# Mixed network on one Trainium2 core: the second tails of the expert rows written at the dense network's chunks 0 to 3 in place of 1, 3, 5 and 7

## The chip, the cores and the metric

One core of a Trainium2 chip runs the whole program. The metric is the time of one execution on the device in microseconds; runs are repeated and their median is compared.

## What is computed

The reference takes 16 sequences of 256 tokens with 128 features and passes them through four residual layers: a linear attention with two decays, a mixture of experts, a retention, and two layers of local attention with a gated feed-forward. The change lies in the mixture of experts, which is in short:

```python
probs = softmax(x_flat @ Wr.T)
topk_scores, topk_experts = top_k(probs, 2)            # two experts a token
y_fb = _ffn(x_flat, fw1, fb1, fw2, fb2)                # the dense network, for overflowing tokens
for e in range(8):
    idx = the first cap tokens that chose e            # cap = 1.25 * T * 2 / 8 = 1280
    y_e = _ffn(x_flat[idx], W1[e], b1[e], W2[e], b2[e])
    y_flat = y_flat.at[idx].add(y_e * w[:, None])
    y_flat = where(overflow, y_fb, y_flat)
```

## The kernel before

All 4096 tokens stay on the chip, features in the partitions, as the residual `XT` and the normed input `H`, in 8 chunks of 512 tokens. The mixture of experts is three blocks of code (`experts`): `routing`, `expert_layers`, `combine`. Each block is one program per engine, and a barrier of all engines closes it.

`routing` (L614) does four things.

- It loads the weights of the nine networks (eight experts and the dense one) and splits each in a high and a low part.
- It computes the routing on VectorE: for each token its two experts, their scores `w1` and `w2`, and the two row numbers `dst` in a table `expert_slots` in DRAM.
- It brings the tokens' rows to DRAM. `tok_rows` has one row of 130 numbers per token: 128 features, the weight, and the address at which the expert's result goes back. GpSimd (L720 to L727) issues 64 indirect DMAs, called scatters below, of 128 rows each: first the 32 blocks of tokens for the first choice (`c` = 0), then the same 32 for the second (`c` = 1). Between the passes the rows differ only in their last two columns. `tail(c, q)` (L829) writes these two columns for the quarter `q`, eight blocks of tokens, with two small copies on VectorE (L831, L832), and counts `tails`. GpSimd waits for `tails` before each group of eight scatters. Since the second tail overwrites the first, it must wait until the first pass's eight scatters of that quarter have landed; that is the semaphore `sent[0][q]`.
- It runs the dense network over the 8 chunks, three matmuls for each product (high and low parts, L689 and L705). ScalarE applies the Gelu (`Gf`, L766) and copies the overflow mask (`WEf`, L774), VectorE splits the result (`Gf_hi` L854, `Gf_lo` L856) and the next input (`Hf_lo` L842), and closes a chunk with `Zf` (L866) and the addition to `XT` (L869). The work is a pipeline: VectorE closes chunk c after splitting chunk c+1, TensorE puts chunk c+1's first product ahead of chunk c's second.

The four tails of the first pass are written before the dense network starts. Those of the second stand in VectorE's program behind the closing of a chunk, and that is where the change is:

```python
                    V.tensor_tensor(k.XT[:, chunk(c)], k.XT[:, chunk(c)], Z[:], ALU.add).then_inc(added, 1)
                    if c % 2:
                        dve.wait_ge(sent[0][c // 2], 16 * 8)
                        tail(1, c // 2)
```

Engines execute their programs in order, and the order is the one written. At the end of `routing` GpSimd waits for all scatters of the second pass, and `expert_layers` (L875) begins with the load of the first expert's rows (`xin`, L901) on SyncE's queue.

Of the kernel before, what the change touches and what calls it, by code (L numbers as in the profile page):

```python
# [58 lines left out]
def chunk(c):  # L59
    return bass.ds(c * CH, CH)  # L60
# [553 lines left out]
def routing(k, w, wide):  # L614
# [3 lines left out]
    with ExitStack() as ctx:  # L618
# [23 lines left out]
        sent = [[sem(f"sent{c}_{q}") for q in range(4)] for c in range(2)]  # L642
# [5 lines left out]
        @block.sync  # L648
        def _(sp):
            for i, (n, e) in enumerate(pieces):  # L650
                if i >= 4:
                    sp.wait_ge(w_lo, i - 3)
                part = k.dram[n][:, e, :] if n == "w1e" else k.dram[n][:, e, :, :].rearrange("p a b -> p (a b)")
                sp.dma_start(raw[:, i % 4, :], part).then_inc(raw_in[i % 4], 16)
                if i < 2:
                    sp.dma_start(w[("b1e", "b2e")[i]][:], k.dram[("b1e", "b2e")[i]]).then_inc(small_in, 16)
            sp.wait_ge(small_in, 32)
# [118 lines left out]
        @block.vector  # L776
        def _(dve):
            V = nc.vector
            done = [0]

            def after(ins):

                done[0] += 1
                ins.then_inc(step, 1)
                dve.wait_ge(step, done[0])

            dve.wait_ge(k.late_in, 16 * N_LATE)
            V.memset(fb, 0.0)
            V.memset(one, 1.0)
            V.memset(before[:, 0:1], 0.0)  # L790
            dve.wait_ge(logit_mm, 1)
            lg = ps[0][:, 0:NT * NE].rearrange("p (n e) -> p n e", e=NE)
            after(V.tensor_reduce(mx, lg, AX.X, ALU.max))
            V.tensor_tensor(pr[:], lg, bc(mx), ALU.subtract).then_inc(shifted, 1)
            dve.wait_ge(exped, 1)
            after(V.tensor_reduce(sm, pr[:], AX.X, ALU.add))
            after(V.reciprocal(rs_, sm))
            after(V.tensor_tensor(pr[:], pr[:], bc(rs_), ALU.mult))
            for p_, v_, hot in ((p1, v1, oh1), (p2, v2, oh2)):
                after(V.tensor_reduce(p_, pr[:], AX.X, ALU.max))  # L800
                after(V.tensor_tensor(eq[:], pr[:], bc(p_), ALU.is_equal))
                after(V.tensor_tensor(val[:], eq[:], r["iota8"][:], ALU.mult))
                after(V.tensor_reduce(v_, val[:], AX.X, ALU.min))
                after(V.tensor_tensor(hot[:], r["iota8"][:], bc(v_), ALU.is_equal))
                if hot is oh1:
                    after(V.scalar_tensor_tensor(pr[:], oh1[:], -2.0, pr[:], ALU.mult, ALU.add))
            after(V.tensor_tensor(oh[:], oh1[:], oh2[:], ALU.add))

            for e in range(NE):
                V.tensor_tensor(elig[:], oh[:, :, e], fb, ALU.is_gt).then_inc(elig_r, 1)  # L810
                dve.wait_ge(elig_r, 2 * e + 1)
                V.tensor_tensor_scan(before[:, 1:NT + 1], one, elig[:], 0.0, ALU.mult, ALU.add).then_inc(elig_r, 1)
                dve.wait_ge(counted, e + 1)
                after(V.scalar_tensor_tensor(over, ps[1][:, e * NT:(e + 1) * NT], float(CAP), elig[:], ALU.is_gt, ALU.mult))
                after(V.tensor_tensor(fb, fb, over, ALU.max))

            after(V.tensor_tensor(val[:], ps[1][:, 0:NE * NT].rearrange("p (e n) -> p n e", n=NT), r["slotbase"][:], ALU.add))
            for c, hot in enumerate((oh1, oh2)):
                after(V.tensor_tensor(eq[:], val[:], hot[:], ALU.mult))
                after(V.tensor_reduce(slot, eq[:], AX.X, ALU.add))  # L820
                after(V.scalar_tensor_tensor(dst[:, c, :], fb, float(NE * CAP), slot, ALU.mult, ALU.add))
            after(V.tensor_copy(fbb[:], fb))
            after(V.tensor_tensor(sm, p1, p2, ALU.add))
            after(V.tensor_scalar(sm, sm, 1e-9, None, ALU.max))
            after(V.reciprocal(rs_, sm))
            V.tensor_tensor(w1, p1, rs_, ALU.mult)
            after(V.tensor_tensor(w2, p2, rs_, ALU.mult))

            def tail(c, q):  # L829
                cc = slice(8 * q, 8 * q + 8)  # L830
                V.tensor_copy(tok[:, cc, P:P + 1].rearrange("p n o -> p (n o)"), (w1, w2)[c][:, cc])  # L831
                V.tensor_copy(tok[:, cc, P + 1:P + 2].rearrange("p n o -> p (n o)").bitcast(mybir.dt.uint32),  # L832
                              r["tokid"][:, c, cc]).then_inc(tails, 1)

            dve.wait_ge(tok_sb, NCH)
            for q in range(4):
                tail(0, q)
            dve.sem_inc(routed, 1)

            def split_low(c):  # L840
                dve.wait_ge(h_hi, c + 1)
                V.tensor_tensor(Hp[1][:, c % 2, :], k.H[:, chunk(c)], Hp[0][:, c % 2, :].bitcast(F32),  # L842
                                ALU.subtract).then_inc(h_lo, 1)

            split_low(0)
            split_low(1)
            for i in range(NCH + 1):
                if i < NCH:
                    for j in range(NJ):
                        n = NJ * i + j  # L850
                        dve.wait_ge(gelu, n + 1)
                        if i > 1 and j == 0:
                            dve.wait_ge(y_mm, i - 1)
                        V.tensor_scalar(Gp[0][:, i % 2, j, :], G[:, j, :], 1.0, None, ALU.mult).then_inc(g_hi, 1)  # L854
                        dve.wait_ge(g_hi, n + 1)
                        V.tensor_tensor(Gp[1][:, i % 2, j, :], G[:, j, :], Gp[0][:, i % 2, j, :].bitcast(F32),  # L856
                                        ALU.subtract).then_inc(g_lo, 1)
                    if i + 2 < NCH:
                        split_low(i + 2)
                if i > 0:  # L860
                    c = i - 1
                    dve.wait_ge(y_mm, c + 1)
                    dve.wait_ge(mask_sb, c + 1)
                    if c > 0:
                        dve.wait_ge(added, c)
                    V.scalar_tensor_tensor(Z[:], ps[4 + c % 2][:], w["b2e"][:, NE:NX], WE[:, c % 2, :],  # L866
                                           ALU.add, ALU.mult).then_inc(z_r, 1)
                    dve.wait_ge(z_r, c + 1)
                    V.tensor_tensor(k.XT[:, chunk(c)], k.XT[:, chunk(c)], Z[:], ALU.add).then_inc(added, 1)  # L869
                    if c % 2:  # L870
                        dve.wait_ge(sent[0][c // 2], 16 * 8)
                        tail(1, c // 2)


def expert_layers(k, w, wide):  # L875
# [1104 lines left out]
```

## Time and profile before

| | before |
|---|---|
| median of 3 runs | 1860.79 us |
| lowest and highest | 1853.89 and 1862.79 us |
| profiled execution, its own time | 1877.42 us |
| its span | 1875.6 us |
| TensorE busy | 1393.1 us (74%) |
| VectorE busy | 1249.4 us (67%) |
| ScalarE busy | 869.0 us (46%) |
| GpSimd busy | 729.5 us (39%) |
| granted TensorE clock, mean | 0.87 |

The durations come from one profiled execution; a difference worked out from them is set against the median of the others. The shares are means over stages of different kind, so they say little about one block. Of use are the order of time of one engine, with the idle time before each instruction and what ended it, and the table of stretches. The engines are written PE (TensorE), PEld (its weight loads), DVE (VectorE), ACT (ScalarE), POOL (GpSimd) and SP (SyncE); a q behind the name is the engine's queue.

### The profile page before, as it was taken

Reading aid. Unit: us, or ns where it says so; the run is one execution under the profiler, and the core shown is the slowest. Engines: PE = TensorE matmul, PEld = TensorE weight load, DVE = VectorE, ACT = ScalarE, POOL = GpSimd, SP = SyncE. Lnnn points to the kernel's source line nnn. Section 1 sums busy time; section 2 is a strip of 40 time slices with the busy share of each in tenths; the row PEclk is TensorE's granted clock in tenths of the full one; section 3 lists DMA queues with packets and bytes.
Section 4 is the critical chain, followed back from the end, with each engine's and each line's share of the span. In section 5 each row is a group of like instructions: output and inputs, shape, how many; then the busy total and the mean of one; then the engine's idle time right before and its main releaser. Section 6 shows DMA issues by size and latency. Waiting matters only on the chain. (4 is left out here: it accounts for less than half of the span.)

```text
span 1875.6 us, 24395 instructions
## 1 busy us (share of the span) xinstructions
PE 1393.1 (74%) x6912; PEld 885.8 (47%) x6912; DVE 1249.4 (67%) x2733; ACT 869.0 (46%) x1621; POOL 729.5 (39%) x588
## 2 busy tenths in 40 slices
PE   7756563674639882874888888888758888888887
PEld 3222121253428671322566666663336666667533
DVE  1598988337538771536988888844469888887343
ACT  6411111443325540563566666654326666666543
POOL 0287778026635553224433333301145333332000
PEclk9867776876669995985899999999959999999898
DMA  5400000021121214000000000000000000000001
GB/s 158 145 0 0 0 0 0 0 69 57 41 70 48 61 47 125 8 0 18 1 2 2 0 0 1 0 25 0 17 1 1 2 2 1 1 1 0 1 0 45
DMA packets 50658, 44.44 MB, mean 24 GB/s; under 512 B 5870, under 2 KB 43763, under 8 KB 50560
## 3 DMA queue, kind: packets, MB, share of 16 engines
q1 hardware_dynamic: 45952, 34.91, 6.4%
q0 software_dynamic: 4608, 8.47, 1.4%
q8 instruction: 32, 0.52, 0.1%
q14 instruction: 66, 0.54, 0.1%
HBM read 23.28 MB, written 21.12 MB: 24 GB/s over the span
## 5 line engine op out<-in xcount | busy, mean ns | idle before, releaser
L1385 POOL TENSOR_TENSOR R<-R 128x512 f32<-128x512 f32 x128 | 159.4, 1266 | 400.3 <-DVE R L1658 400.3
L1658 DVE TENSOR_TENSOR R<-bank,tab 128x1024 f32<-128x1024 f32 x128 | 151.6, 1221 | 55.4 <-ACT sq L1561 47.4
L1392 POOL TENSOR_TENSOR R<-R,rn 128x512 f32<-128x512 f32 x128 | 139.9, 1114 | 12.1 <-issue 10.0
L1498 PE MATMUL bank<-PT,VA 128*128 128x192 f32 x512 | 137.8, 352 | 0.0
L1561 ACT ACTIVATE sq<-bank 128x512 f32<-128x512 f32 x128 | 76.2, 597 | 122.4 <-PE bank L1410 117.3
L1436 PE MATMUL bank<-ident,R 128*128 128x128 f32 x512 | 85.3, 293 | 64.0 <-ACT VA L1584 61.9
L1677 DVE TENSOR_SCALAR QKr<-QK 128x512 fp32r<-128x512 f32 x128 | 92.6, 751 | 48.5 <-ACT QK L1577 47.0
L1034 POOL DMA_INDIRECT expert_rows<-Yt,xin x80 | 83.2, 1041 | 92.2 <-DVE Yt L1007 67.9
L1697 DVE TENSOR_TENSOR OT<-bank,rd 64x256 f32<-64x256 f32 x256 | 106.3, 415 | 19.1 <-ACT rd L1603 16.5
L1595 ACT ACTIVATE PT<-bank 128x320 f32<-128x320 f32 x256 | 98.0, 435 | 16.4 <-PE bank L1486 13.5
L1436 PEld LDWEIGHTS bank<-ident,R 128*128 128x128 f32 x512 | 61.6, 147 | 90.8 <-issue 47.0
L395 PE MATMUL bank<-phk,spread 128*128 128x512 f32 x64 | 45.9, 883 | 77.7 <-DVE phq L445 77.7
L463 DVE TENSOR_TENSOR_SCAN S<-beta,U 128x512 f32<-128x512 f32 x64 | 101.8, 1600 | 1.1
L1499 PE MATMUL bank<-PT,VA 128*128 128x128 f32 x512 | 101.0, 280 | 0.0
L1410 PE MATMUL bank<-wqkv_hi,hs_hi 128*128 128x512 f32 x128 | 62.9, 492 | 48.2 <-DVE hs_lo L1645 40.6
L1499 PEld LDWEIGHTS bank<-PT,VA 128*128 128x128 f32 x512 | 93.8, 197 | 0.0
L1688 DVE CUSTOM_DVE_ANT_0 masked<-bank,mask_q 128x192 bf16<-128x192 f32 x256 | 89.9, 351 | 0.0
L1577 ACT ACTIVATE QK<-bank 128x512 f32<-128x512 f32 x128 | 75.7, 593 | 26.0 <-PE bank L1436 26.0
L1498 PEld LDWEIGHTS bank<-PT,VA 128*128 128x128 f32 x512 | 81.6, 198 | 9.5 <-issue 6.7
L1601 ACT ACTIVATE rd<-bank 64x512 f32<-64x512 f32 x128 | 75.9, 593 | 17.0 <-PE bank L1499 14.2
L1603 ACT ACTIVATE rd<-rd 64x512 f32<-64x512 f32 x128 | 80.7, 630 | 4.1
L723 POOL DMA_INDIRECT expert_slots<-tok_rows,dst x64 | 64.4, 1006 | 43.7 <-DVE tok_rows L832 25.5
(306 smaller groups left out, 3877.2 us busy)
## 6 DMA issues: line engine op xcount, KB each, us to landing
expert_slots<-empty SPq DMA_DIRECT2D x8, 650.0 KB, 6.5
xin<-expert_slots SPq DMA_DIRECT2D x8, 650.0 KB
expert_rows<-empty SPq DMA_DIRECT2D x8, 512.0 KB, 6.7
Ye<-expert_rows SPq DMA_DIRECT2D x16, 256.0 KB, 5.3
expert_raw<-w1e_dram SPq DMA_DIRECT2D x9, 256.0 KB, 2.9
expert_raw<-w2e_dram SPq DMA_DIRECT2D x9, 256.0 KB, 3.0
tok<-x_dram SPq DMA_DIRECT2D x8, 256.0 KB, 4.6
out_dram<-tok_out SPq DMA_DIRECT2D x8, 256.0 KB, 3.3
```

Source lines behind the costliest of these rows:

```text
L463: nc.vector.tensor_tensor_scan(S[i % 2][:], beta[m][:, chunk(c)], U[d][:], 0.0, ALU.mult, ALU.add).then_inc(s_scan, 1)
L1034: nc.gpsimd.indirect_dma_start(k.ys[:, :], bass.IndirectOffsetOnAxis(ap=ids, axis=0), Yt[:, s % 3, t, :], None, bounds_check=2 * T - 1, oo ...
L1385: nc.gpsimd.tensor_tensor(halves[:, :, 0, :, z, :], halves[:, :, 0, :, z, :], halves[:, :, 1, :, 1 - z, :], ALU.add).then_inc(summed, 1)
L1392: nc.gpsimd.tensor_tensor(x, x, scale.to_broadcast([P, HEADS, DH]), ALU.mult).then_inc(normed, 1)
L1436: m = nc.tensor.transpose(ps[bank][:, b * P:(b + 1) * P], R[:, t % 2, qk, 0, b * P:(b + 1) * P], k.const["ident"][:])
L1498: nc.tensor.matmul(bank[:, o:o + KW], VA[par][:, 2 * s, h, :], pt[:, 0:KW], start=True, stop=True)
L1499: nc.tensor.matmul(bank[:, o + P:o + SEQ], VA[par][:, 2 * s + 1, h, :], pt[:, KW:KW + P], start=False, stop=True, skip_group_check=True).t ...
L1595: nc.scalar.activation(PT[:, u % 4, :], ps[BT + u % 2][:, 0:KW + P], ACT.Exp, scale=QK_SCALE).then_inc(pt_r, 1)
L1658: nc.vector.tensor_tensor(R[:, i, qk, :, :].rearrange("p c (h d) -> p c h d", d=DH), x, y.to_broadcast([P, 2, HEADS, DH]), ALU.mult).then_ ...
L1677: nc.vector.tensor_scalar(QKr[cc], QK[par][cc], 1.0, None, ALU.mult).then_inc(qkr_r, 1)
L1688: nc.vector.tensor_tensor_reduce(masked[:, v % 2, KW:2 * KW], bank[:, KW:2 * KW], mask[:, KW:2 * KW], -1.0, FAR, ALU.add, ALU.min, nm[:, 2 ...
L1697: m = nc.vector.tensor_tensor(OT[par][i * DH:(i + 1) * DH, b, s * SEQ:(s + 1) * SEQ], ps[BO + p % 2][0:DH, i * SEQ:(i + 1) * SEQ], rd[:, p ...
```

## The change

The second tails are written behind chunks 0, 1, 2 and 3 of the dense network, one quarter each, where they stood behind chunks 1, 3, 5 and 7.

```diff
@@ -867,9 +867,9 @@
                     V.tensor_tensor(k.XT[:, chunk(c)], k.XT[:, chunk(c)], Z[:], ALU.add).then_inc(added, 1)
-                    if c % 2:
-                        dve.wait_ge(sent[0][c // 2], 16 * 8)
-                        tail(1, c // 2)
+                    if c < 4:
+                        dve.wait_ge(sent[0][c], 16 * 8)
+                        tail(1, c)
```

On VectorE, behind the closing of chunk 0 in the dense network (a minus is a row of before alone, a plus one of the change; `cols` holds the scores, `tokid` the addresses):

```order
 L866 SCALAR_TENSOR_TENSOR Zf<-bank,b2e,WEf 128x512
 L869 TENSOR_TENSOR XT<-XT,Zf 128x512
+L831 COPY tok_rows<-cols 128x8
+L832 COPY tok_rows<-tokid 128x8
 L854 TENSOR_SCALAR Gf_hi<-Gf 128x512
 L856 TENSOR_TENSOR Gf_lo<-Gf,Gf_hi 128x512
```

The two copies of the first quarter now stand ahead of the splitting of chunk 2. The same piece stands behind chunk 2 for the third quarter. Behind chunks 1 and 3 the rows read the same before and after, though the quarter is another one: the second in place of the first, the fourth in place of the second.

On VectorE, behind the closing of chunk 7, at the end of the block (L618 is the block's end):

```order
 L866 SCALAR_TENSOR_TENSOR Zf<-bank,b2e,WEf 128x512
 L869 TENSOR_TENSOR XT<-XT,Zf 128x512
-L831 COPY tok_rows<-cols 128x8
-L832 COPY tok_rows<-tokid 128x8
 L618 UNCONDITIONAL_BRANCH
```

The last quarter's copies have left this place, and those behind chunk 5 likewise. The order on the other engines is unchanged.

## Rows read from the trace of the kernel before

**Rows 1.** Table of stretches: busy time of each engine, clock, DMA.
```profile
core 0: us, PE busy (x) PEld busy (x) DVE busy (x) ACT busy (x) POOL busy (x), PEclk, DMA share, GB/s
445.00:462.00 17.00, 16.44 (x68) 12.71 (x68) 11.95 (x20) 6.79 (x11) 12.95 (x13) 0.87 0.14 46
462.00:492.00 30.00, 7.38 (x18) 4.07 (x18) 7.35 (x12) 4.42 (x7) 19.21 (x20) 0.57 0.14 45
492.00:527.00 35.00, 32.44 (x140) 24.24 (x139) 32.97 (x65) 17.16 (x29) 21.73 (x22) 0.93 0.12 40
527.00:552.00 25.00, 0.00 (x0) 0.00 (x0) 0.00 (x0) 0.00 (x0) 10.50 (x11) 0.52 0.22 63
```
**Rows 2.** POOL in order of time: start, us, instruction, idle before and releaser.
```profile
445.39 1.67 POOL L723 DMA_INDIRECT expert_slots<-tok_rows,dst  x1 [12.98 <-DVE tok_rows L832]
...
455.27 0.97 POOL L723 DMA_INDIRECT expert_slots<-tok_rows,dst  x1 [0.30 <-issue]
...
486.03 0.97 POOL L723 DMA_INDIRECT expert_slots<-tok_rows,dst  x1 [0.30 <-issue]
493.81 1.12 POOL L723 DMA_INDIRECT expert_slots<-tok_rows,dst  x1 [6.81 <-DVE tok_rows L832]
...
507.74 1.12 POOL L723 DMA_INDIRECT expert_slots<-tok_rows,dst  x1 [3.59 <-DVE tok_rows L832]
...
520.16 1.12 POOL L723 DMA_INDIRECT expert_slots<-tok_rows,dst  x1 [2.08 <-DVE tok_rows L832]
...
539.57 0.97 POOL L723 DMA_INDIRECT expert_slots<-tok_rows,dst  x1 [0.30 <-issue]
```
**Rows 3.** The block's end, line L618: duration in ns min/median/max, start in us.
```profile
L618 DVEq DRAIN  x1: 879/879/879, 526.0 to 526.0; - x1
...
L618 POOLq DRAIN  x1: 5285/5285/5285, 542.5 to 542.5; - x1
```
**Rows 4.** All engines in order of time, from 540 us on.
```profile
547.98 2.92 SPq L901 DMA_DIRECT2D xin<-expert_slots  x3
...
552.35 0.90 PE L913 MATMUL bank<-ident,xin 128*128 128x128 f32 x3 [27.63 <-DMA xin<-expert_slots]
```
**Rows 5.** DVE in order of time.
```profile
462.44 0.75 DVE L866 SCALAR_TENSOR_TENSOR Zf<-bank,b2e,WEf 128x512 f32<-128x512 f32 x1 [3.29 <-PE bank L705]
...
491.40 0.75 DVE L866 SCALAR_TENSOR_TENSOR Zf<-bank,b2e,WEf 128x512 f32<-128x512 f32 x1 [5.32 <-remote]
...
492.87 0.17 DVE L832 COPY tok_rows<-tokid 128x8 uint32<-128x8 uint32 x1
...
497.88 0.74 DVE L866 SCALAR_TENSOR_TENSOR Zf<-bank,b2e,WEf 128x512 f32<-128x512 f32 x1
...
505.33 0.75 DVE L866 SCALAR_TENSOR_TENSOR Zf<-bank,b2e,WEf 128x512 f32<-128x512 f32 x1 [0.83 <-remote]
...
525.22 0.75 DVE L866 SCALAR_TENSOR_TENSOR Zf<-bank,b2e,WEf 128x512 f32<-128x512 f32 x1
...
526.69 0.17 DVE L832 COPY tok_rows<-tokid 128x8 uint32<-128x8 uint32 x1
```
**Rows 6.** ACT in order of time.
```profile
466.67 0.69 ACT L766 ACTIVATE Gf<-bank,b1e 128x512 f32<-128x512 f32 x1 [11.61 <-remote]
470.96 0.69 ACT L766 ACTIVATE Gf<-bank,b1e 128x512 f32<-128x512 f32 x1 [3.60 <-remote]
...
483.59 0.69 ACT L766 ACTIVATE Gf<-bank,b1e 128x512 f32<-128x512 f32 x1 [5.62 <-remote]
...
490.60 0.60 ACT L774 ACTIVATE WEf<-bank 128x512 f32<-128x512 f32 x1 [5.81 <-remote]
491.45 2.42 ACT L766 ACTIVATE Gf<-bank,b1e 128x512 f32<-128x512 f32 x4 [0.25 <-remote]
```
**Rows 7.** PE in order of time: first and last matmul of chunk 2's first product, 12 in all.
```profile
456.03 0.39 PE L689 MATMUL bank<-Hf_hi,w1e_hi 128*128 128x512 f32 x1
...
458.59 0.40 PE L689 MATMUL bank<-Hf_hi,w1e_lo 128*128 128x512 f32 x1
```
**Rows 8.** Waits of ACT over the whole span: us in total, times, longest.
```profile
ACT Yf L974 <- remote: 35.6, 7, 8.6
```

## The prediction, made before the kernel was run

> **What bounds the kernel at this place.** I read the table of stretches first [rows 1]. The dense network runs from 445 to 527 us of the span, TensorE, VectorE and ScalarE are empty from 527 to 552, and GpSimd alone still works there. The program ends each block of code with a barrier of all engines, so the question is who arrives last. GpSimd's order of time answers it [rows 2]: it issues 64 scatters of rows, in a first pass of 32 (445.39 to 487.00) and a second of 32 that it begins at 493.81 and ends at 540.54. Its drain takes 5.29 us [rows 3], the queue issues the first load of the experts at 547.98, and TensorE, idle for 27.63 us, starts at 552.35 [rows 4]. From the end of the last scatter to that load it is 7.4 us. All later work stands behind that load, so a microsecond won or lost at the barrier is one of the kernel's.
>
> The second pass has holes. GpSimd waits for VectorE's second tails (weight and address of the rows) for 6.81 us, 3.59 us and 2.08 us; the fourth tail is in time [rows 2]. A scatter costs 0.30 us of idling in any case, so the holes are worth 12.48 - 3 x 0.30 = **11.6 us**. That is all that writing tails earlier can give.
>
> Why are tails late? VectorE's rows [rows 5] give the chunk's first closing operation (Zf): chunk 0 at 462.44, chunk 1 at 491.40, chunk 2 at 497.88, chunk 3 at 505.33, chunk 7 at 525.22. Between chunks 2 to 7 it is 5.5 us on average; between 0 and 1 it is 29 us. In those 29 us ScalarE's Gelus and one copy come one at a time, 4 to 7 us apart, at 466.67, 470.96, 483.59 (one more lies between) and 490.60, and then four follow without a pause [rows 6]. The matmuls that they wait for were shown long before: chunk 2's group runs from 456.03 to 458.98 and needs nothing more, while the Gelu on its first bank starts at 466.67 [rows 6, 7]. So TensorE's results become known late, one by one, in this stretch. GpSimd scatters without a pause from 445.39, the results are first late after some 10.6 us of that (456.03), and all are released by 491.40, 4.4 us after the last scatter of the pass ended. The wait that the profile calls "remote" falls where GpSimd scatters, also in the expert layers (7 waits of Yf, 35.6 us) [rows 8]. I read this as one fact: a long stream of scatters holds TensorE's results up, and a pause in the stream releases them. Why it does is not in the rows.
>
> **The change, step by step.** It moves two copies of 128x8 each (0.17 us each in rows 5) and one wait, four times, on VectorE alone; no other engine's order changes, and nothing is added.
>
> 1. *Tail 1 goes from behind chunk 1 to behind chunk 0.* Its wait is for the first eight scatters, the last of which was issued at 455.27 and generated by 456.2 [rows 2]. Bounding the landing by the drain, 5.3 us [rows 3], it is satisfied by 461.5; chunk 0 closes at 462.44. No stall, and the tail is written at 464, long before GpSimd wants it at 487.3. The first hole closes: group 1 of the second pass runs from 487.3 to 497.6 (eight scatters take 10.3 us, from 41.6 us for 32 in the first pass and 20.4 us for 16 at the end).
> 2. *Tail 2 goes from behind chunk 3 to behind chunk 1.* In before, chunk 1 closed at 491.40 because the stream had stopped. Now the stream goes on to 497.6. If the release needs the stop, chunk 1 closes at 497.6 + 4.4 = 502.0, its tail is ready 1.6 us later (as 491.40 to 493.04) and GpSimd starts 0.8 us after that (493.04 to 493.81), at 504.4. **A hole of 6.8 us stands again, one group later.** Group 2 runs to 514.7. If instead chunk 1 still closes at 491.40, or by 496, there is no hole.
> 3. *Tail 3, from behind chunk 5 to behind chunk 2.* Chunk 2 follows chunk 1 by 6.5 us [rows 5]: 508.5, tail 510.1, before 514.7. No hole; group 3 runs from 515.0 to 525.3.
> 4. *Tail 4, from behind chunk 7 to behind chunk 3.* Chunk 3 follows chunk 2 by 7.45 us: 515.9 if nothing is late. But the stream that began at 504.4 reaches 10.6 us of age at 515.0, just then. The ends are 515.9 and 525.3 + 4.4 = 529.7. The tail stands at 517.5 to 531.3, so group 4 starts between 525.6 and 532.1 and ends between 535.9 and 542.4. With the 7.4 us up to the load: 543.3 to 549.8.
> 5. *The rest of the network.* In before it takes 21.5 us from chunk 3's Zf to the last tail (505.33 to 526.86) [rows 5], and VectorE's drain 0.9 us [rows 3]. Counted from 515.9 or 529.7 the network is at the barrier at 538.3 or 552.1. Its cover, the 21 us by which VectorE was early at the barrier, is used up at the late end.
>
> Sum: the load goes out at the later of both, 543.3 to 552.1 against 547.98, which is **-4.7 to +4.1 us**, centre 0. The waits that the change adds on VectorE cost nothing in this sum: each asks for eight scatters of the first pass, over by 487.0 and landed by 492.3, while chunk 1 closes at 491.4 or later and chunk 3 far behind. What queues behind such a wait is chunk c+1's Gf_hi, and TensorE waits for that.
>
> **Against the median.** The profiled execution took 1877.42 us (span 1875.6), 16.6 us above the median of 1860.79. The sum is a difference, and I take it from the median: 1860.8 + 0, said as **1861 us**.
>
> **Rivals.**
> - *N, nothing was late outside the profiled execution.* The 16.6 us may include the late results themselves; the rows cannot tell. Then chunks follow at 6.5 us from chunk 0's 462.4 on, the four tails of before stand at 470.5, 483.5, 496.5 and 509.5 and are wanted at 487, 498, 508 and 518: GpSimd has no hole to close. After the change VectorE waits for landings in chunks 1 to 3, until about 492 at most; chunks 4 to 7 add 26 us, 518, still ahead of GpSimd's 528. The change does nothing: 0 us, 1861.
> - *F, all the holes close.* Chunks 1, 2 and 3 closed at 491.4, 497.9 and 505.3 in before; group ends are 497.6, 507.9 and 518.2. If the network keeps its own pace whatever GpSimd issues, all tails are in time and the full 11.6 us come: 1849.2. For it: the release at 490.60 also fits the 6 to 7 us steps before it and need not come from the stop. Against it: in one step after 490.60 everything was free, which a plain step does not explain. The Trainium skill, SBUF — State Buffer, § Who interferes with whom, supports F: it says that only VectorE and GpSimd share ports and that TensorE and ScalarE never wait on anyone. By that rule the scatters would not hold up TensorE and the sum would be -11.6 us; rows 6 and 7 do not look like it.
> - *S, slower: the network is held one chunk per group.* If results are late again sooner than 6.5 us into group 2 (the deciding point: chunk 2 not closed by about 513), then chunk 2 closes at 514.7 + 4.4 = 519.1, group 3 starts at 521.5 and stops at 531.8, chunk 3 closes at 536.2, group 4 ends at 548.9 and the load goes out at 556.3; the network is at the barrier at 536.2 + 21.5 + 0.9 = 558.6. That is +10.6 us, 1871.4. For it: groups now follow each other with shorter pauses, so the hold-up may not empty. Against it: in before, 2 to 3.6 us of pause between groups kept chunks at 7.5 us or less.
>
> **How the numbers follow.** My case has 0.40, N 0.25, F 0.17, S 0.18. A measurement of this kernel can tell about 0.5%, 9.3 us, from no change. F is over it by 2 us only and S by 1.3, so each gives its side about 0.12 and leaves the rest within; the edges of my case add 0.03 to faster and 0.06 to slower. Faster 0.15, same 0.67, slower 0.18. The range reaches to F at 1849 and to S at 1872: beyond it lies half of F and of S.
>
> **What would show it.** In the profile after: the first second-pass scatter directly behind the 32nd of the first (idle 0.30 us); then one hole of 5 to 8 us before the 9th, ended by L832; chunk 1's Zf near 502 and not 491; the last scatter's end between 536 and 543. Zf of chunk 1 at 491 or before with scatters unbroken to 528 would be F. Three holes again, with chunk 2 behind 513, would be S. If the load stands earlier in the profile but the median does not move, N is right. I am wrong altogether if VectorE idles before L831 for a landing, or if a later stretch changes its length.

## The result: 0.3% slower, with one hole in place of three

| | before | changed kernel |
|---|---|---|
| median of 20 runs each | 1859.15 us (1853.89 to 1867.22) | 1866.55 us (1857.50 to 1871.15) |
| ratio to before, 95% interval | | 1.0030 (1.0019 to 1.0041), about +5.6 us |
| profiled execution, its span | 1877.42, 1875.6 | 1867.42, 1865.1 |
| granted TensorE clock, mean of the span | 0.870 | 0.873 |
| first load of the experts | 547.98 | 552.46 |

By the prediction's measure of 0.5% this is no difference; the interval says that it is a small loss all the same. The profiled execution of after is shorter than that of before by 10 us while the median is longer by 7: the experts' layers after the load took 176.3 us in the profiled execution of before and 163.3 us in this one (from the load to the end of that block), and the change touches nothing there. So spans are not compared below, but the place where the load goes out.

The stretches of the changed kernel, in the columns of [rows 1] (length, busy time and instructions of PE, PEld, DVE, ACT and POOL, granted clock, DMA share, GB/s):

```profile
445.00:462.00 17.00, 16.16 (x68) 12.67 (x68) 13.75 (x26) 6.71 (x11) 12.67 (x13) 0.87 0.13 43
462.00:492.00 30.00, 9.81 (x24) 5.36 (x23) 5.31 (x11) 3.86 (x6) 22.99 (x24) 0.58 0.16 52
492.00:527.00 35.00, 24.52 (x89) 16.76 (x89) 19.11 (x39) 10.85 (x18) 21.62 (x22) 0.74 0.13 42
527.00:552.00 25.00, 13.66 (x46) 9.16 (x45) 14.08 (x24) 6.64 (x11) 6.80 (x7) 0.64 0.07 22
```

The last stretch, in which before had only GpSimd at work, now holds the end of the dense network: TensorE is busy for 13.66 us of it. GpSimd's scatters, the four that matter (against [rows 2]):

```profile
486.58 0.97 POOL L723 DMA_INDIRECT expert_slots<-tok_rows,dst  x1 [0.30 <-issue]
...
496.79 0.97 POOL L723 DMA_INDIRECT expert_slots<-tok_rows,dst  x1 [0.30 <-issue]
504.90 1.12 POOL L723 DMA_INDIRECT expert_slots<-tok_rows,dst  x1 [7.15 <-DVE tok_rows L832]
...
534.83 0.97 POOL L723 DMA_INDIRECT expert_slots<-tok_rows,dst  x1 [0.30 <-issue]
```

The second pass follows the first without a hole, one hole of 7.15 us stands before its ninth scatter, and the last scatter ends at 535.80 (before: 540.54). GpSimd is 4.7 us earlier. The network is not. VectorE's closing operations of chunks 1, 2, 3, 4, 5 and 7 (against [rows 5]):

```profile
502.49 0.75 DVE L866 SCALAR_TENSOR_TENSOR Zf<-bank,b2e,WEf 128x512 f32<-128x512 f32 x1 [23.45 <-remote]
...
508.98 0.74 DVE L866 SCALAR_TENSOR_TENSOR Zf<-bank,b2e,WEf 128x512 f32<-128x512 f32 x1
...
515.50 0.74 DVE L866 SCALAR_TENSOR_TENSOR Zf<-bank,b2e,WEf 128x512 f32<-128x512 f32 x1
...
531.84 0.75 DVE L866 SCALAR_TENSOR_TENSOR Zf<-bank,b2e,WEf 128x512 f32<-128x512 f32 x1 [9.73 <-remote]
...
542.80 0.74 DVE L866 SCALAR_TENSOR_TENSOR Zf<-bank,b2e,WEf 128x512 f32<-128x512 f32 x1
...
550.70 0.75 DVE L866 SCALAR_TENSOR_TENSOR Zf<-bank,b2e,WEf 128x512 f32<-128x512 f32 x1 [0.78 <-PE bank L705]
```

Chunk 4 comes 16.3 us behind chunk 3. In before that step had no wait. ScalarE shows the same two hold-ups (against [rows 6]), each ended some 3 to 5 us after GpSimd's last scatter of a run (497.76 and 535.80), with several Gelus at once:

```profile
502.54 2.42 ACT L766 ACTIVATE Gf<-bank,b1e 128x512 f32<-128x512 f32 x4 [16.98 <-remote]
...
519.16 0.60 ACT L774 ACTIVATE WEf<-bank 128x512 f32<-128x512 f32 x1 [2.87 <-remote]
534.65 0.69 ACT L766 ACTIVATE Gf<-bank,b1e 128x512 f32<-128x512 f32 x1 [14.90 <-remote]
538.88 1.84 ACT L766 ACTIVATE Gf<-bank,b1e 128x512 f32<-128x512 f32 x3 [3.54 <-remote]
```

The drains of the block's end, and then the load (against [rows 3, 4]): the three drain figures are minimum, median and maximum in ns, then the start.

```profile
L618 POOLq DRAIN  x1: 5285/5285/5285, 537.6 to 537.6; - x1
...
L618 DVEq DRAIN  x1: 727/727/727, 551.5 to 551.5; - x1
```

```profile
552.46 2.98 SPq L901 DMA_DIRECT2D xin<-expert_slots  x3
...
556.89 1.11 PE L913 MATMUL bank<-ident,xin 128*128 128x128 f32 x4 [6.22 <-DMA xin<-expert_slots]
```

GpSimd is drained at 542.9, VectorE at 552.2. The barrier waited for GpSimd in before; now it waits for the network. That is the load's +4.5 us between the two profiles, and it is most of the measured 5.6.

The waits by name also show where the time of a hold-up is booked (engine, line, releaser; total, times, longest):

```profile
ACT Gf L766 <- remote: 54.7, 7, 17.0
...
DVE Zf L866 <- remote: 34.2, 3, 23.4
...
ACT Yf L974 <- remote: 13.0, 5, 4.0
```

Gf and Zf waited 27.5 and 6.2 us in before and wait 54.7 and 34.2 us now; Yf, in the experts, fell from 35.6 to 13.0 us, which is the profiled execution's own difference named above. What TensorE itself does in a hold-up, from its order of time: the last matmul of chunk 1's second product, and then chunk 2's second product between 488 and 501:

```profile
461.94 0.40 PE L705 MATMUL bank<-Gf_hi,w2e_lo 128*128 128x512 f32 x1
...
489.85 0.59 PE L705 MATMUL bank<-Gf_hi,w2e_lo 128*128 128x512 f32 x1 [0.81 <-issue]
492.65 0.59 PE L705 MATMUL bank<-Gf_hi,w2e_hi 128*128 128x512 f32 x1 [2.21 <-issue]
495.45 0.59 PE L705 MATMUL bank<-Gf_lo,w2e_hi 128*128 128x512 f32 x1 [2.21 <-issue]
498.25 0.59 PE L705 MATMUL bank<-Gf_hi,w2e_lo 128*128 128x512 f32 x1 [2.21 <-issue]
500.35 0.59 PE L705 MATMUL bank<-Gf_hi,w2e_hi 128*128 128x512 f32 x1 [1.51 <-issue]
```

From 489.85 to 498.25 it is one matmul in 2.8 us, its weight load in between, so one instruction in 1.4 us; the matmuls of the same product just before (485.99 to 487.41) follow each other at 0.42 to 0.57 us. The idle time is put down to "issue", a wait for nothing that the profile shows. The step shortens again with this weight load, 0.70 us behind the matmul at 498.25 and 1.2 us after the scatters stopped:

```profile
498.95 0.29 PEld L705 LDWEIGHTS bank<-Gf_hi,w2e_hi 128*128 128x128 f32 x1 [1.82 <-issue]
```

So two things happen. Finished results become known late, as the prediction had it, and this is what chunk 1 waited for: its last matmul began at 461.94 and its Zf started at 502.49, 40 us later. On top of that, TensorE's instructions are spaced out after a while, here those of chunk 2. Before the spacing began TensorE had run ahead of the results that were known: by an estimate from the order of the matmuls, 32 lay between the last known result (the mask of chunk 1, copied at 484.97) and the last one at full pace (487.41), and 33 at the second hold-up (519.16 and 521.17).

### The profile page after: what moved, and what is told of

Same layout as the page of the kernel before. It is cut to its first block and busy times, and to the rows that moved or that the text cites. A ratio compares the mean times of both kernels' runs of the same rounds, so it can differ in the third digit from the quotient of the medians.

```text
span 1865.1 us, 24395 instructions
## 1 busy us (share of the span) xinstructions
PE 1393.6 (75%) x6912; PEld 887.2 (48%) x6912; DVE 1251.2 (67%) x2733; ACT 869.0 (47%) x1621; POOL 727.4 (39%) x588
## 5 line engine op out<-in xcount | busy, mean ns | idle before, releaser
L1595 ACT ACTIVATE PT<-bank 128x320 f32<-128x320 f32 x256 | 98.0, 435 | 16.6 <-PE bank L1486 13.8
L1686 DVE CUSTOM_DVE_ANT_0 masked<-bank,mask_q 128x128 bf16<-128x128 f32 x256 | 73.0, 285 | 11.8 <-issue 4.8
```

The lines of the kernel that those rows point to most:

```text
L1595: nc.scalar.activation(PT[:, u % 4, :], ps[BT + u % 2][:, 0:KW + P], ACT.Exp, scale=QK_SCALE).then_inc(pt_r, 1)
```

## Experiments

Twelve runs in five series. Each series ran on another chip, with runs of before on the same chip beside it. The theory after the result, called **held up**: a long unbroken stream of scatters holds TensorE up (its results are known late and, later on, its instructions are spaced out), and the change exchanges two short pauses for a second hold-up. Rivals: **pace** (the scatters have nothing to do with it, the network is slow there), **landing** (what counts is the transfers in flight, not the stream of issues) and **null** (nothing is late in most executions).

**1. Before, once more, with a profile.**

> The kernel before once more, for a second trace. Theory A (a stream of scatters holds TensorE up; the changed kernel is slower because its network now ends last at the barrier): the first load of the experts at 548 us of the span again, chunk 1's Zf at 491, and the experts' block of code, 176 us in the first trace of before and 163 us in the trace after, is near 163 us here, so that the first trace of before was an outlier there. Rival B (the change shortens the experts' block by 13 us and something else costs more): 176 us again.

Measured 1846.97 us; the median of before beside it on that chip was 1845.53 us (11 runs), not 1860. VectorE, GpSimd, and the load:

```profile
457.28 0.74 DVE L866 SCALAR_TENSOR_TENSOR Zf<-bank,b2e,WEf 128x512 f32<-128x512 f32 x1
463.83 0.74 DVE L866 SCALAR_TENSOR_TENSOR Zf<-bank,b2e,WEf 128x512 f32<-128x512 f32 x1
...
497.38 0.75 DVE L866 SCALAR_TENSOR_TENSOR Zf<-bank,b2e,WEf 128x512 f32<-128x512 f32 x1
```

```profile
491.30 0.97 POOL L723 DMA_INDIRECT expert_slots<-tok_rows,dst  x1 [0.30 <-DVE tok_rows L832]
...
525.81 0.97 POOL L723 DMA_INDIRECT expert_slots<-tok_rows,dst  x1 [0.30 <-issue]
```

```profile
533.94 2.99 SPq L901 DMA_DIRECT2D xin<-expert_slots  x3
```

The same program on another chip has no late result at all: chunks 6.5 us apart, no wait for "remote" anywhere in its list of waits, the 64 scatters without a hole, the load 14.0 us earlier. Its stretch from 462 to 492, in the columns used above:

```profile
462.00:492.00 30.00, 28.54 (x136) 21.19 (x134) 29.22 (x58) 17.21 (x28) 22.99 (x24) 1.00 0.16 52
```

Same 24 scatters, same DMA share and GB/s as in after's row of that stretch, but 136 matmuls against 24, and the granted clock at 1.00, the level of 2.4 GHz, where the changed kernel's TensorE idled for two thirds of the stretch and had 0.58. Theory A's places of the load (548) and of chunk 1's Zf (491) were missed; its 163 us for the experts' block came out as 157.8. This split the question in two: what holds TensorE up, and where it happens. Below, a chip with hold-ups is one where the median of before lies near 1860 us, as in the result, and not near 1845. Each chip was met in one series only, so a chip and its session are not told apart.

**2. One unbroken stream: GpSimd writes the second tails itself (on before).**

```diff
                     if n % 8 == 0:
+                        if c:
+                            q = n // 8
+                            pool.wait_ge(sent[0][q], 16 * 8)
+                            nc.gpsimd.tensor_copy(tok[:, n:n + 8, P:P + 1].rearrange("p n o -> p (n o)"), w2[:, n:n + 8])
+                            nc.gpsimd.tensor_copy(tok[:, n:n + 8, P + 1:P + 2].rearrange("p n o -> p (n o)").bitcast(mybir.dt.uint32),
+                                                  r["tokid"][:, 1, n:n + 8]).then_inc(tails, 1)
                         pool.wait_ge(tails, 4 * c + n // 8 + 1)
...
-                    if c % 2:
-                        dve.wait_ge(sent[0][c // 2], 16 * 8)
-                        tail(1, c // 2)
```

> GpSimd writes the second tails itself, so that no scatter waits for VectorE and the 64 scatters are one stream. Theory A: TensorE is held from about 456 us to the end of the stream; scatters end at about 535 us (82 us, plus four pairs of small copies), chunk 1's Zf comes 4 to 5 us after that, about 539, and the remaining six chunks take some 36 us: load of the experts at about 575, 27 us later than in before, time about 1886 us, if the hold-up is there in timed runs too. Rival F (the network keeps its pace): the load at about 542, time 6 us under before. Rival N (the hold-up is of the profiled execution only): 1886-like spans in the profile, but timed runs at or under before's.

Measured 1850.12 us (8 runs), ratio 1.0032 (1.0015 to 1.0048). GpSimd pays for the copies at each group (here 0.79 us instead of 0.30 before a group, and the copies):

```profile
488.64 0.28 POOL L725 COPY tok_rows<-cols 128x8 f32<-128x8 f32 x1
488.87 0.39 POOL L726 COPY tok_rows<-tokid 128x8 uint32<-128x8 uint32 x1
490.05 1.08 POOL L729 DMA_INDIRECT expert_slots<-tok_rows,dst  x1 [0.79 <-POOL tok_rows L726]
```

From its first scatter to the load it is 93.9 us, 90.4 in experiment 1: the copies cost 3.6 us, within the interval of 2.8 to 8.9. There was no hold-up here, so it said nothing of one.

**3. No scatters at all (on before).**

```diff
-            for c in range(2):
-                for n in range(NT):
-                    if n % 8 == 0:
-                        pool.wait_ge(tails, 4 * c + n // 8 + 1)
-                    nc.gpsimd.indirect_dma_start(k.xs[:, :], bass.IndirectOffsetOnAxis(ap=dst[:, c, n:n + 1], axis=0),
-                                                 tok[:, n, :], None, bounds_check=NE * CAP - 1,
-                                                 oob_is_err=False).then_inc(sent[c][n // 8], 16)
-            for q in range(4):
-                pool.wait_ge(sent[1][q], 16 * 8)
...
-                    if c % 2:
-                        dve.wait_ge(sent[0][c // 2], 16 * 8)
-                        tail(1, c // 2)
```

> Without any scatter into the experts' slots, and without second tails: the experts work on empty slots, their part of the result is left out. Theory A: no result of TensorE is late in this block; chunk 1's Zf at 466 to 469 us, chunks 6 us apart, chunk 7 closed by 510, the load of the experts at 512. Rival (ScalarE or code loading holds the network between 456 and 491 us, whatever GpSimd does): chunk 1's Zf at 491 again.

Measured 1806.52 us, one run. The first load of the experts goes out at 495.47 instead of 533.94, since GpSimd no longer comes last; these 38.5 us account for the 39.0 by which the time fell. Theory A had the load at 512 and chunk 1's Zf at 466 to 469 (462.06 here). The chunks are 6.25 us apart instead of 6.54, so on this chip the scatters slow the network by 0.3 us a chunk, 4 to 5%. From 460 to 490 us TensorE's matmuls of L689 take the same in both (392 to 398 ns); VectorE's splitting does not, 460 against 421 ns for Gf_hi and 714 against 693 for Gf_lo, which is 0.24 us of the 0.3 over a chunk's four banks.

**4. The changed kernel with a wait for the landing after every eight scatters.**

```diff
                                                  oob_is_err=False).then_inc(sent[c][n // 8], 16)
+                    if n % 8 == 7:
+                        pool.wait_ge(sent[c][n // 8], 16 * 8)
```

> The changed kernel with one wait more: GpSimd waits after each eight scatters until they have landed. Theory A with a short pause that suffices: seven pauses of some 1.5 us, the network is never held for long, chunk 1's Zf before 475, last scatter ends at 538 to 540, load at about 546: 2 us under before, 6 to 8 us under the changed kernel. Theory A with a pause that has to be 4 us long: chunk 1's Zf still behind 490, load at 553 to 560, slower than the changed kernel. Rival (the release had nothing to do with pauses): times as in the changed kernel plus the pauses, some 10 us.

Measured 1859.93 us (4 runs), ratio 1.0073 (1.0053 to 1.0093). Seven holes like this one:

```profile
455.87 1.36 POOL L723 DMA_INDIRECT expert_slots<-tok_rows,dst  x1 [2.13 <-DMA expert_slots<-tok_rows,dst]
```

A landing is known 1.8 us later than the next scatter could start (2.1 against 0.30). Seven of them make 12.8 us; 0.73% is 13.5. It is the price of a pause for every group, on a chip that needs none; whether such pauses release anything could not show here.

**5, 6. The changed kernel, and experiment 2's stream, in a second series.**

> The changed kernel again, beside before on whatever chip this is. In the last job the trace of before had no late result at all (chunks 6.5 us apart from 457 us on, the load at 533.7) and its median was 1845.5, not 1859. Theory C (the hold-up belongs to some chips or sessions and is in the timed runs there): if before's median is near 1845 here, the network of the changed kernel is in time too, the load stands at 533 to 534 and the ratio is 1.000 within 0.1%; if before's median is near 1859, chunk 1's Zf comes some 5 us after a pause of the scatters, the load at 550 to 555, ratio 1.003. Rival D (the change costs some 0.3% by itself, by its waits or by order): ratio 1.003 also where nothing is late.

> GpSimd writes the second tails itself, one stream of scatters. It was 1.0032 of before on the chip without late results (load at 540.0 against 533.7: the copies on GpSimd). Theory C: the same again if before's median is near 1845; if it is near 1859, TensorE is held to the end of the stream, the load at 570 to 580 and the time 20 us or more over before. Rival (the hold-up comes at random and has nothing to do with the stream): about 6 us over before in either case.

Before had 1844.27 us here (23 runs). The changed kernel: 1843.54 us (12 runs), ratio 0.9999 (0.9982 to 1.0016). The stream: 1848.06 us (10 runs), ratio 1.0015 (0.9995 to 1.0034). No hold-up on this chip either. What the changed kernel does here, VectorE first, then GpSimd's last scatter:

```profile
465.82 0.18 DVE L831 COPY tok_rows<-cols 128x8 f32<-128x8 f32 x1 [1.45 <-DMA expert_slots<-tok_rows,dst]
...
476.21 0.18 DVE L831 COPY tok_rows<-cols 128x8 f32<-128x8 f32 x1 [3.83 <-DMA expert_slots<-tok_rows,dst]
...
486.24 0.18 DVE L831 COPY tok_rows<-cols 128x8 f32<-128x8 f32 x1 [3.47 <-DMA expert_slots<-tok_rows,dst]
```

```profile
525.12 0.97 POOL L723 DMA_INDIRECT expert_slots<-tok_rows,dst  x1 [0.30 <-issue]
```

VectorE now reaches the tails before the first pass has landed and waits 8.75 us in all, but nobody waits for VectorE: the scatters run without a hole and the load goes out 90.5 us after the first scatter, against 90.4. This is the rival "null" on this chip, and it speaks against rival D: by its waits and order alone the change costs nothing measurable. (The loads that the expectations here and below quote as 533.7, 540.0 and 495.3 read 533.94, 540.45 and 495.47 in the traces.)

**7, 8. The stream and the kernel without scatters, a third series.**

> The one-stream kernel once more, to meet a chip on which TensorE's results are late. Theory C: if before's median is near 1859 here, chunk 1's Zf comes only behind the last scatter, the load of the experts at 570 to 580 and the time at least 20 us over before; if it is near 1845, the load at 540 and 3 to 6 us over before, as twice already. Rival (random, not tied to the stream): 3 to 6 us over before in either case.

> No scatters into the slots, no second tails; that part of the result is left out. On the chip without late results the load stood at 495.3 and the chunks were not held. Theory C: the same here, 495 to 497, even if before's median is near 1859. Rival (on the slow chip TensorE is held in this block whatever GpSimd does): chunk 1's Zf behind 480, the load at 520 or later.

Before had 1860.74 us here (7 runs, 1859.05 to 1864.37): a chip with hold-ups. The stream: 1880.35 us (4 runs, 1877.84 to 1882.84), ratio 1.0102 (1.0080 to 1.0124), where the two other chips gave 1.0032 and 1.0015. Its chunks 1, 2 and 3 on VectorE, the first matmul of chunk 3 on TensorE, chunk 3's first three Gelus, and the load:

```profile
499.72 0.75 DVE L872 SCALAR_TENSOR_TENSOR Zf<-bank,b2e,WEf 128x512 f32<-128x512 f32 x1 [31.50 <-remote]
...
534.31 0.74 DVE L872 SCALAR_TENSOR_TENSOR Zf<-bank,b2e,WEf 128x512 f32<-128x512 f32 x1
...
540.55 0.75 DVE L872 SCALAR_TENSOR_TENSOR Zf<-bank,b2e,WEf 128x512 f32<-128x512 f32 x1
```

```profile
457.89 0.39 PE L689 MATMUL bank<-Hf_hi,w1e_hi 128*128 128x512 f32 x1
```

```profile
508.12 0.69 ACT L772 ACTIVATE Gf<-bank,b1e 128x512 f32<-128x512 f32 x1 [35.10 <-remote]
516.52 0.69 ACT L772 ACTIVATE Gf<-bank,b1e 128x512 f32<-128x512 f32 x1 [7.71 <-issue]
524.92 0.69 ACT L772 ACTIVATE Gf<-bank,b1e 128x512 f32<-128x512 f32 x1 [7.71 <-issue]
```

```profile
561.45 3.01 SPq L904 DMA_DIRECT2D xin<-expert_slots  x3
```

Two chunks, 0 and 1, closed in 86 us of stream (scatters from 441.52 to 527.64); chunk 2 closes 6.7 us behind the last scatter and chunks 3 to 6 follow at 5.6 to 6.3 us each. Chunk 3's first bank is written by three matmuls from 457.89 to 458.76 and its Gelu starts at 508.12, 49 us later. The next two Gelus come 8.40 us apart, and each needs three matmuls and three weight loads more: results, too, become known at one instruction in 1.4 us. Theory C had the direction right and overstated the size: it wanted chunk 1 only behind the last scatter (it closed at 499.72, in the middle of them), the load at 570 to 580 (561.45) and 20 us or more (19.6). The load is 119.9 us behind the first scatter, 26.0 more than the same program in experiment 2. In the same series the kernel without scatters took 1814.52 us (one run), its load went out at 492.84 (theory C: 495 to 497), and its VectorE shows chunks 6.24 us apart and no wait for a result:

```profile
459.46 0.75 DVE L857 SCALAR_TENSOR_TENSOR Zf<-bank,b2e,WEf 128x512 f32<-128x512 f32 x1
465.71 0.74 DVE L857 SCALAR_TENSOR_TENSOR Zf<-bank,b2e,WEf 128x512 f32<-128x512 f32 x1
```

This kernel took 8.0 us more here than in experiment 3, though its load went out 2.6 us earlier: 5.0 us lie in the experts' block (163.3 against 158.2), where GpSimd scatters as well and ScalarE's Yf waits 13.4 us for "remote", and the rest behind it. So the two kinds of chip differ outside the dense network too.

In this block, on a chip with hold-ups, the network runs freely when nothing is scattered, and hardly at all under an unbroken stream. That refutes "pace" and shows the first half of "held up". The three kernels order themselves by their pauses there: before with three (1), the changed kernel with one (1.0030, from the series of the result), the stream with four of 0.8 us (1.0102). These are two series, and the stream also pays for its copies, 0.15 to 0.32% where nothing is held up; 0.7 to 0.9% are left for the longer hold-up.

**9 to 12. Pauses put where before has them, in a fourth and a fifth series.** On before, GpSimd waits ahead of groups 3 to 6 until the network has passed a given chunk:

```diff
                         pool.wait_ge(tails, 4 * c + n // 8 + 1)
+                        g = 4 * c + n // 8
+                        if g in (2, 3, 4, 5):
+                            pool.wait_ge(h_mm, NJ * (3, 5, 6, 7)[g - 2])
```

> Before, with four waits more on GpSimd: the scatter groups 3 to 6 of the eight each wait until the first product of the dense network's chunk 2, 4, 5 and 6 is known. Theory C: on a chip without late results each wait is satisfied when it is reached (by 464, 475, 485 and 495 us of the span) and the ratio is 1.000. On a chip with late results GpSimd stops after 20 us of stream in place of 42, the held-up results are few and come 1 to 4 us after the stop, so that holes of 2 to 5 us stand where one of 6.8, one of 3.6 and one of 2.1 stood; chunk 1's Zf before 480, last scatter at 536 to 541, load at 543 to 548: 0 to 5 us under before. Rival (the hold-up lasts until a long stop): more holes of 5 us and more, load behind 550.

> The changed kernel with a wait for landing after every eight scatters. Without late results it cost 14 us (load at 547.8). If this chip has late results (before near 1859): Theory with short pauses: holes of 1.8 us keep the results in time, the network closes chunk 7 by 515, the load at 548 again, within 2 us of before. Theory with long pauses only: chunk 1's Zf behind 485 and the load behind 555.

> Before, for a second trace on a chip where results are late, if this is one: the load at 546 to 549, chunk 1's Zf at 489 to 492, and the experts' block 160 to 177 us. On a chip without: the load at 533 to 534 and the experts' block 158 us.

> The paced kernel once more, to meet a chip with late results. Theory C: if before's median is near 1859, holes of 2 to 5 us in the scatters, chunk 1's Zf before 480, the load at 543 to 548, 0 to 5 us under before; if before's median is near 1845, ratio 1.000 within 0.1%, as in the last run. Rival (only a long stop releases the results): on the slow chip the load behind 550 and the kernel slower than before.

Neither chip had hold-ups: before 1845.38 us (17 runs) and 1844.13 us (17 runs), its profile 1847.23 us with the load at 536.00. The paced kernel: 1843.13 us, ratio 0.9993 (0.9976 to 1.0010), and 1845.31 us, ratio 1.0006 (0.9988 to 1.0023), 12 runs each. Its waits are over when GpSimd comes to them:

```profile
465.71 0.97 POOL L726 DMA_INDIRECT expert_slots<-tok_rows,dst  x1 [0.30 <-PE bank L689]
...
487.89 0.97 POOL L726 DMA_INDIRECT expert_slots<-tok_rows,dst  x1 [0.30 <-DVE tok_rows L835]
```

They cost nothing measurable on such a chip. The kernel with landings repeated its loss: 1855.47 us (4 runs), ratio 1.0066 (1.0046 to 1.0086). Whether paced waits gain on a chip with hold-ups stays untested: neither series met one. The same holds of "landing": short pauses of 2.1 us were never run where TensorE is held up, so issues and transfers in flight are not told apart.

## Why the prediction was right, and where it was not

The time was forecast as 1861, and measured at 1859.15 x 1.0030 = 1864.7 when taken against the runs of before, 1866.55 as a plain median: inside the range, and "same". The range of 1849 to 1872 is wide enough for many ways to the same number, so the steps say more:

- **Steps 1 and 2 held.** The first hole closed. The second came back one group later, 7.15 us at 504.90 (forecast 6.8 at 504.4), and chunk 1 closed at 502.49 (502.0), 4.7 us after the stop (4.4 assumed). The reading behind them, that finished results become known late under the scatters, is borne out by the 40 us between chunk 1's last matmul and its Zf; the spacing of TensorE's instructions was not in it. Of the rivals, F wanted chunk 1 at 491 and no hole: false here. By the rule cited for it (the Trainium skill, SBUF — State Buffer, § Who interferes with whom: TensorE and ScalarE never wait on anyone) the sum was -11.6 us; the rows at 502.49 and 499.72, with 23.45 and 31.50 us of waiting, disagree with what was drawn from it, while the profiles from chips without hold-ups agree with it: the 0.3 us a chunk of experiment 3 are mostly VectorE's, and TensorE's matmuls take the same with and without scatters.
- **Step 3 and step 4 held at their early end.** Chunks 2 and 3 at 508.98 and 515.50 (508.5, 515.9), last scatter over at 535.80 (535.9), so GpSimd alone would have let the load go at 543.2.
- **Step 5 failed: "In before it takes 21.5 us from chunk 3's Zf to the last tail."** Up to the end of VectorE's drain it took 36.7 us (515.50 to 552.2). The 21.5 us were read where scatters came in groups with holes of 3.6 and 2.1 us between them; after the change, groups 2 to 4 are one stream of 30.9 us (504.90 to 535.80) under just these chunks. I had set a clock of 10.6 us for a stream to become harmful, and used it for chunk 3 and not for what follows chunk 3: WEf was late from 519.16 on, 14.3 us into the stream, and the mask that it copies had been written at 514.06, 9.2 us into it, so that clock was about right and not carried on. With the network held again the barrier's last comer changed. 552.46 is just over the late end of 552.1, reached by another way than the one that bounded it: chunk 3 in time, chunk 4 late. That it lies so near the bound is luck. (The bound itself is 0.9 us too high: VectorE's drain ran from 526.0 to 526.9 in before, so it is within the 21.5 us up to 526.86 and was counted twice.)
- **S** had the right sign and a right reason (shorter pauses do not empty the hold-up), but its deciding point, chunk 2 later than 513, was missed by 4 us, and its +10.6 was twice the loss.
- **N** is what happens where nothing is held up: 0.9999 on the one such chip that ran the changed kernel, and before itself shows no late result in the profiles of two. Its argument was right that a program without lateness has no hole to close; its setting was wrong. It depends on the chip or the session, not on the one profiled execution: on the chips with hold-ups the timed runs have them as well, since the stream's four runs there (1877.84 to 1882.84) all stand some 30 us above those of the same program elsewhere. The sign I gave for "wrong altogether", VectorE idling before L831 for a landing, is found where nothing is held up (1.45, 3.83 and 3.47 us in experiment 5) and costs nothing.
- **Against the median.** The 16.6 us between the profiled execution and the median of before were mostly the experts' block, 176.3 us against 163.3, 162.4 and 163.3 in the three other profiles of chips with hold-ups and 157.8 in experiment 1. To take the sum as a difference was right.

Why does the old placement do better there? Behind chunks 1, 3, 5 and 7 a tail is written only when the network has got so far. When TensorE is held up the tails are late, GpSimd has to stop, and the stop, as I read it, is what frees TensorE. By this reading the three holes, 11.6 us, looked like loss and worked as a brake. Where nothing is held up the tails are early and the brake is off. That the holes cause the release is supported by the releases behind the stops at 487.00, 497.76, 527.64 and 535.80; it was not tried by adding pauses alone on such a chip. A stop is not needed for every result either: chunk 4 of the changed kernel (531.84) and chunk 1 of the stream (499.72) closed while scatters were still going out, only far too late.

**Still open:** why scatters delay TensorE's results and space out its instructions, why on some chips and not on others (of the numbered ones 11 did, 4, 7, 8 and 12 did not), whether issues or transfers in flight do it, and whether the paced version would beat both kernels on such a chip. The changed kernel itself met hold-ups in one series only, so its +0.3% there is not repeated. And every run here has its span and granted clock on record, so none tells whether results would be late without that recording. No version was found that is measurably faster than before.

## What to carry to other kernels

A hole in one engine's order of time may be what keeps another engine going. Before closing it, look at what ran freely during it, and do not price the work behind the change by a duration that was read under the old pauses. When two executions differ by 1% without a change, look for the wait that only one of them has, and repeat on other chips before an effect of 0.3% is explained.

## What the runs showed of the hardware that was not expected

- One program, two behaviours by chip or session: before at 1844.1 to 1845.5 us on four chips and at 1859 to 1861 us in two series, with "remote" waits in the profiles of the latter alone. Of the 14.0 us between the loads of two profiles of before (533.94 and 547.98) 12.2 lie between the first scatter and the load (90.4 and 102.6). The experts' block is longer as well: 162.4 to 163.3 us in three profiles of chips with hold-ups and 176.3 in the fourth, 157.3 to 158.2 in the ten others.
- During a hold-up TensorE's results become known at one instruction in 1.4 us, up to 49 us late (458.76 to 508.12 in the stream), and its own instructions start no faster once it is some 32 matmuls ahead. GpSimd's scatters keep their 0.97 us and 0.30 us between them. The granted clock was 0.50, the lower level of 1.2 GHz, in the stream's stretch from 475 to 492 us, where TensorE was busy for 5.38 of 17 us.
- In the dense network it came only after a run of scatters: the first late result was written 10.6 us into the first stream of before (456.03) and 9.2 us into the second one of the changed kernel (514.06 behind 504.90). TensorE's instructions came closer again 1.2 us after the stop (498.95 behind 497.76), and the next chunk closed 4.4, 4.7 and 6.7 us behind it (491.40, 502.49, 534.31).
- The landing of a scatter is known 1.8 us after the next could have started; GpSimd's drain at the block's end took 5.285 us before and after the change, and 5.287 in the three streams.
